# Deformable convolution on one core: bilinear weights read from a PSUM bank, the first corner add in two instructions

## The reference

```python
om = conv3x3(x, w_om, b_om)                       # offsets dy, dx and a mask for 9 taps
y0, x0 = floor(py), floor(px); fy, fx = py - y0, px - x0
sampled = corner(y0, x0, (1-fy)*(1-fx)) + corner(y0, x0+1, (1-fy)*fx) \
        + corner(y0+1, x0, fy*(1-fx)) + corner(y0+1, x0+1, fy*fx)
sampled = sampled * sigmoid(m)[:, None]
y = einsum('bckhw,ock->bohw', sampled, w) + b
x = x + relu((y - bn_mean) * scale + beta)
```

## Time and profile before

| | |
|---|---|
| three runs, median | 1822.37 us (1814.28 to 1834.46) |
| the profiled execution, its own time | 1817.64 us |
| its span in the trace | 1815.7 us |
| granted TensorE clock, mean | 0.87 of full speed |

### The profile page before, as it was taken

One profiled execution on the slowest core, in us unless ns is written; L12 is line 12 of the kernel. 1 busy time (PEld: TensorE's weight loads), 2 busy tenths in 40 slices (PEclk: granted clock), 3 DMA queues, 4 the chain that ended last, 5 costly groups with the idle time before them and its releaser, 6 DMA issues.

```text
span 1815.7 us, 13011 instructions
## 1 busy us (share of the span) xinstructions
PE 1335.5 (74%) x3820; PEld 578.4 (32%) x3820; DVE 921.6 (51%) x1344; ACT 522.2 (29%) x861; POOL 1240.9 (68%) x1393
## 2 busy tenths in 40 slices
PE   1867674896259998864599998754799754886986
PEld 1543232343124343322244333321343221332422
DVE  2345456454533435887434338975243596333165
ACT  1212121221123343211423442223234313223344
POOL 8367777767777777777777777777777777770000
PEclk9888886898579999986699999976799886997998
DMA  7022323332352222323342223222311122211000
GB/s 231 20 71 62 88 64 76 102 89 65 83 118 54 54 57 64 83 58 82 83 105 53 58 56 81 70 62 70 103 50 51 51 71 54 61 53 30 0 1 12
DMA packets 111189, 122.37 MB, mean 67 GB/s; under 512 B 50704, under 2 KB 88336, under 8 KB 110736
## 3 DMA queue, kind: packets, MB, share of 16 engines
q0 software_dynamic: 36864, 75.57, 15.6%
q1 hardware_dynamic: 73296, 42.57, 9.7%
q10 hardware_dynamic: 960, 3.41, 0.5%
HBM read 99.79 MB, written 9.08 MB: 60 GB/s over the span
## 4 chain that ended last, share of the span: by engine, by line
POOL 53%; PE 19%; issue 17%; DVE 4%; DMA 2%; SPq 2%; ACT 2%; ACTq 0%; POOLq 0%; DVEq 0%
POOL gt L936 53%; PE bank L1567 3%; PE bank L1563 3%; PE bank L1577 3%; PE bank L1688 2%; PE bank L1651 2%; PE bank L1597 2%; PE bank L1638 2%; DMA sqb<-gate_of_token 1%; PE bank L1674 1%; DVE gt L1365 1%; SPq L680 1%; PE bank L1626 1%; SPq L722 1%; DMA gate_of_token<-cw 0%
## 5 line engine op out<-in xcount | busy, mean ns | idle before, releaser
L936 POOL DMA_INDIRECT gt<-corner_table,idx x1152 | 1187.3, 1031 | 387.5 <-issue 350.2
L1365 DVE TENSOR_TENSOR gt<-gt,cw 128x1152 f32<-128x1152 f32 x128 | 173.6, 1356 | 153.7 <-DMA gt<-corner_table,idx 153.2
L1638 PE MATMUL bank<-u,wk 128*128 128x512 f32 x512 | 242.2, 618 | 11.7 <-DMA u<-sqb 6.5
L1651 PE MATMUL bank<-yg,wts 128*128 128x512 f32 x512 | 237.3, 608 | 0.3 <-DVE rb L1406 0.3
L1567 PE MATMUL bank<-xg,w_sb 128*128 128x512 f32 (+1 forms) x288 | 144.9, 587 | 82.2 <-DVE xg L1278 74.5
L1449 DVE SCALAR_TENSOR_TENSOR rb<-xp,par,rb 128x1024 f32<-128x1024 f32 x151 | 187.7, 1291 | 0.0
L1394 DVE SCALAR_TENSOR_TENSOR tg<-tg,ae 128x512 f32<-128x512 f32 x64 | 44.3, 693 | 242.6 <-ACT ae L1078 242.6
L1616 PE MATMUL bank<-cst,sm 128*128 128x128 f32 x384 | 76.7, 316 | 114.3 <-DVE sm L1371 111.8
L1287 DVE SCALAR_TENSOR_TENSOR he<-he,bank 128x512 f32<-128x512 f32 (+1 forms) x144 | 90.2, 627 | 128.8 <-PE bank L1567 123.7
L1006 ACT ACTIVATE he<-bank 128x512 f32<-128x512 f32 (+1 forms) x144 | 79.1, 549 | 248.5 <-PE bank L1563 248.1
L1563 PE MATMUL bank<-xp,w_sb 128*128 128x512 f32 (+1 forms) x288 | 142.3, 578 | 4.0 <-ACT he L1006 3.4
(11 more groups left out here) (186 smaller groups left out, 1257.5 us busy)
## 6 DMA issues: line engine op xcount, KB each, us to landing
gt<-corner_table,idx POOLq DMA_INDIRECT x1152, 2.6
tb<-gate_of_token SPq DMA_DIRECT2D x32, 256.0 KB, 5.1
sqb<-gate_of_token SPq DMA_DIRECT2D x24, 256.0 KB, 5.1
u<-sqb SPq DMA_DIRECT2D x48, 128.0 KB, 6.5
corner_table<-tb SPq DMA_DIRECT2D x36, 128.0 KB, 2.5
w_sb<-w ACTq DMA_DIRECT2D x2, 1024.0 KB, 6.7
sqb<-gate_of_token SPq DMA_DIRECT2D x16, 128.0 KB, 3.2
out<-X SPq DMA_DIRECT2D x8, 256.0 KB, 2.2
```

The costliest lines, as they stand in the source:

```text
L936: pool.indirect_dma_start(gt[:, t % GRING, k].rearrange("p a c -> p (a c)"), None, corners, bass.IndirectOffsetOnAxis(ap=idx[s % 2][:, j, ...
L1365: ch.then(tt(rows, rows, share.unsqueeze(2).to_broadcast([P, 4 * KK, C]), ALU.mult))
L1638: op = mm(psum[b][:, :], wk[:, t, d], u4[:, g, at:at + HALF], start=t == 0, stop=t == JJ - 1 and n > 0)
L1651: op = mm(psum[B2.bank(*name)][:, :], w_glu[:, k, col + d * P:col + (d + 1) * P], yg[:, c % 2, k], start=k == 0, stop=k == NB2 - 1)
```

## The change

Three edits, all in L1.

1. At the first tile of each bunch DVE copies the shares of the whole bunch (4 tiles x 1 or 2 images x 36 values) from `cw` to PSUM bank 4 with a tensor_scalar by 1.0, and each tile's multiplication reads its 36 shares from that bank in place of SBUF. `gt` stays in SBUF.
2. So bank 4 is no longer there for `dcn`: its product, the ReLU and the add to x use bank 3, the bank of the transposed samples, in turn with them.
3. The first corner add, 576 elements, becomes two instructions, of the taps 0 to 4 (320 elements) and 5 to 8 (256), with no wait between them.

```diff
             elif kind == "dcn":
-                use((4,), ("dcn", *k))
+                use((3,), ("dcn", *k))
...
             def dcn(s, m):
                 r = rows(sums(s)[m][0])
+                b = B1.bank("dcn", s, m)
                 B1.filled(act, "dcn", s, m)
-                act.activation(psum[4][r, :], psum[4][r, :], ACT.Relu, bias=bi1[r, :], scale=sc1[r, :])\
+                act.activation(psum[b][r, :], psum[b][r, :], ACT.Relu, bias=bi1[r, :], scale=sc1[r, :])\
                    .then_inc(S["relu_done"], 1)
...
                 rows = gt[:, i].rearrange("p k a c -> p (k a) c")
-                share = cw[s % 2][:, j, g * KK:(g + 1) * KK].rearrange("p k a -> p (k a)")
+                images, n = sums(s)[m]
+                w = len(images) * KK * 4
+                if j % NJ == 0 and g == images[0]:
+                    some = cw[s % 2][:, n * NJ:(n + 1) * NJ, images[0] * KK:(images[-1] + 1) * KK]
+                    ch.then(ts(psum[4][:, 0:NJ * w].rearrange("p (t k) -> p t k", t=NJ),
+                               some.rearrange("p t k a -> p t (k a)"), 1.0, None, ALU.mult))
+                at = (j % NJ * len(images) + images.index(g)) * KK * 4
+                share = psum[4][:, at:at + 4 * KK]
                 ch.then(tt(rows, rows, share.unsqueeze(2).to_broadcast([P, 4 * KK, C]), ALU.mult))
-                ch.then(tt(gt[:, i, :, 0:2], gt[:, i, :, 0:2], gt[:, i, :, 2:4], ALU.add))
+                for ks in (slice(0, 5), slice(5, KK)):
+                    ch.did(tt(gt[:, i, ks, 0:2], gt[:, i, ks, 0:2], gt[:, i, ks, 2:4], ALU.add))
+                ch.wait()
...
             def dcn(s, m):
                 B1.vacant(pe, "dcn", s, m)
+                b = B1.bank("dcn", s, m)
...
-                        op = mm(psum[4][g * C:(g + 1) * C, :], w_dcn[:, k], st[:, place_in(s, m, g), k], start=k == 0,
+                        op = mm(psum[b][g * C:(g + 1) * C, :], w_dcn[:, k], st[:, place_in(s, m, g), k], start=k == 0,
                                 stop=k == 2)
-                op.then_inc(full[4], 1)
+                op.then_inc(full[b], 1)
```

More of the change, by code:

```diff
@@ L1378, in dcn @@
                 xh = X[r, s, n * HALF:(n + 1) * HALF]
-                tt(xh, xh, psum[4][r, :], ALU.add).then_inc(free[4], 1)
+                b = B1.bank("dcn", s, m)
+                tt(xh, xh, psum[b][r, :], ALU.add).then_inc(free[b], 1)
             def l2_head(s, i):
```

## The result

| | before | changed |
|---|---|---|
| median | 1824.8 us (1814.3 to 1834.5) | 1782.3 us (1778.7 to 1783.4) |
| profiled execution | 1817.64 us, span 1815.7 | 1783.39 us, span 1781.6 |
| last indirect DMA ends | 1639.3 us | 1602.0 us |

The ratio is 0.9764 with a 95% interval of 0.9736 to 0.9792: 2.4% faster, where 1.5% was forecast (1795 us, range 1777 to 1816). Between the two profiled executions the difference is 34.3 us.

What follows compares the result with a forecast made beforehand. POOL's 1152 indirect DMAs, each row plus its pause, were taken to bound the kernel. Terms -61.9 + 27.7 + 2.7 + 2.4 + 1.5 = -27.6 us took the median from 1822.4 to 1795 us; own range 1785 to 1803, full range 1777 to 1816.

Steps and rivals of the forecast that it cites:

- part 1: L1's multiplication, reading its shares from PSUM, no longer holds any indirect DMA: -61.9 us.
- Part 2: DMAs let through wait at random moments for the split add and the sum: +27.7 us, bounds -4.9 and +57.8.
- second rival: Adds and sum take back what the multiplication gives, their moments falling badly in each tile: 1813 us, chance 0.12.
- Part 3: In two stretches, some 20 tiles, DMAs let through meet L3's taps and lose half the gain: +2.7 us.
- Part 4: From 287 to 409 us DVE and PE are behind, so POOL waits away its gain in 9 tiles: +2.4 us.
- third rival: DVE and PE become the bound, POOL meets a full ring each step, half the gain lost: 1807 us, chance 0.08.
- Part 5: DVE's extra time for add halves and copies, multiplication unchanged, is mostly covered by waits for gathers: +1.5 us.
- Part 6: Moving dcn to bank 3 costs nothing: 0 taken, upper bound 12 us of PE's time.
- Part 7: After the last gather, the tail of L2 and L3 has no POOL work and moves as a whole, staying 176 us.
- last rival: More gain than counted: the add's halves let DMAs in early and fewer meet the adds: 1777 us, chance 0.07.

Runs made afterwards that it cites:

- e3: Changed kernel with the multiplication reading its shares from cw in SBUF again, all else kept: 1824.4 us, 1.0037 of the kernel before.
- e5: Changed kernel with the first add split by corner, one half written to PSUM for the last add, shares copied per tile: 1783.1 us, 0.9786 of the kernel before.
- e9: Changed kernel with the last add reading one operand from PSUM and the first step's expert units spread over more tiles: 1775.1 us, 0.9748 of the kernel before.
- e6: Changed kernel with the first step's 32 expert units spread over tiles 16.3 to 24.0 instead of 22.5: 1772.7 us, 0.9736 of the kernel before.
- e4: Kernel before with only dcn's product moved to bank 3: 1819.2 us, 0.9999 of the kernel before.
- e8: The changed kernel run again without any edit: 1781.5 us, 0.9785 of the kernel before.
- e1: Changed kernel with the first corner add as one instruction again: 1781.1 us, 0.9802 of the kernel before.
- e10: Changed kernel with the expert units spread over more tiles and the first corner add in one piece: 1771.0 us, 0.9735 of the kernel before.

## Why the prediction was right, and where its sizes were off

The forecast was faster, 1795 us; it is 1782. The mechanism stood as argued: DMAs waited for DVE instructions with two SBUF tensors, and the multiplication's 61.9 us went to zero (part 1). e3 shows the cause by one operand: 88 DMAs held for 51.5 us with it in SBUF, none with it in PSUM. The Trainium skill says that in its probe tensor_tensor did not stall DMAs whose descriptors GpSimd makes (SBUF — State Buffer, section Who interferes with whom); for the indirect DMAs of this kernel these two runs show otherwise.

Part 2, the DMAs that meet the adds, was mis-sized: +27.7 forecast, +5.8 + 2.3 = +8.1 measured. (The squares given there make 32.4 us, not 32.6.) I had used a random moment, and the moments aren't random. In 61 of the 128 tiles of the changed kernel a DMA began in the stretch from 0.20 us before the add to 0.03 after its start and was not held; at random it would be 128 x 0.23 / 1.24 = 24.

One reason can be read from the rows. When a DVE instruction just before the multiplication holds a DMA, that DMA is released as the multiplication starts, and the next one reads 1.24 us later, while the multiplication has 1.35 us to run and the add behind it starts at 1.38. Here a tap does it:

```profile
721.64 1.27 DVE L1460 SCALAR_TENSOR_TENSOR rb<-xp,par,rb 128x1024 f32<-128x1024 f32 x1
722.11 1.62 POOL L936 DMA_INDIRECT gt<-corner_table,idx  x1 [0.30 <-issue]
722.84 1.34 DVE L1373 TENSOR_TENSOR gt<-gt,bank 128x1152 f32<-128x1152 f32 x1
724.04 0.94 POOL L936 DMA_INDIRECT gt<-corner_table,idx  x1 [0.30 <-issue]
724.21 0.83 DVE L1375 TENSOR_TENSOR gt<-gt 128x320 f32<-128x320 f32 x2
```

In 27 of the 61 tiles the DMA before was held in this way. In the other 34 it was not, so this is less than half of the explanation. The last tile but one is of these: DVE had waited 8.07 us for the gather, and nothing stood before the multiplication that could hold a DMA.

```profile
1592.21 1.35 DVE L1373 TENSOR_TENSOR gt<-gt,bank 128x1152 f32<-128x1152 f32 x1 [8.07 <-DMA gt<-corner_table,idx]
1593.43 0.94 POOL L936 DMA_INDIRECT gt<-corner_table,idx  x1 [0.30 <-issue]
1593.60 0.82 DVE L1375 TENSOR_TENSOR gt<-gt 128x320 f32<-128x320 f32 x2
1594.46 0.46 DVE L1381 TENSOR_TENSOR sm<-gt 128x288 f32<-128x288 f32 x1
1594.68 1.05 POOL L936 DMA_INDIRECT gt<-corner_table,idx  x1 [0.30 <-issue]
```

The DMA at 1593.43 passes just ahead of the add, and the one after it falls to the sum and waits 0.11 us. The counts are from the rows; no run moved the moments by themselves, and for the 34 tiles the cause stays open. It was the second rival's idea of regular moments, with the opposite sign. Its lower bound (nothing added) was nearer than the value that I took.

Part 3, the taps, was too small: +2.7 forecast, +8.4 measured. I counted half the gain of some 20 tiles, but more DMAs are held by taps than before (34 against 25), each for longer (0.69 against 0.60 us on average). One of them:

```profile
714.16 1.28 DVE L1460 SCALAR_TENSOR_TENSOR rb<-xp,par,rb 128x1024 f32<-128x1024 f32 x1
714.54 1.72 POOL L936 DMA_INDIRECT gt<-corner_table,idx  x1 [0.30 <-issue]
```

This row is 0.78 us over 0.94. e5 and e9 show it again: with the last add freed as well the taps take 25.1 and 26.9 us.

Part 4, the stretch with the full ring, was too small: +2.4 forecast, +10.2 measured. I had counted the tiles 16 to 24 alone. What POOL had gained in the tiles before was waited for as well, as the starts of the tiles' first DMAs show (tiles counted from 0; us earlier than in the trace of the kernel before):

| tile | 14 | 20 | 26 | 40 | 56 | 127 |
|---|---|---|---|---|---|---|
| changed | 8.9 | 7.6 | 0.2 | 9.2 | 13.7 | 37.3 |
| e6 | 8.9 | 8.4 | 14.9 | 20.2 | 25.8 | 48.8 |

After the stretch (tile 26 begins at about 409 us) the changed kernel has nothing left of its lead. e6 keeps it. The third rival (DVE and PE bound) was right in this one place and nowhere else.

Part 5: sizes right, 0.492 and 0.417 us for the halves, 0.455 and 0.301 for the copies, and no PSUM cost of the multiplication. By the two fixed costs in the Trainium skill (VectorE: DVE Perf Modes, section The TRN2 errata), 120 cycles from PSUM and 58 from SBUF, it would by estimate be 65 ns longer; it is 8 ns shorter. Part 6, bank 3, is nothing, as e4 shows. Part 7, the tail moves as a whole: it took 3.2 us longer, which is within what it varies by.

Parts 2 to 4 together were forecast at +32.8 and are +26.7. That they came so near is partly luck: part 2 was 19.6 us too high, parts 3 and 4 together 13.5 us too low. With the rest of the table the profiled executions differ by -34.3 us, where the sum said -27.6. The medians differ by more, 42.5 us when the result was taken and 41.4 in e8's group, since the profiled execution of the kernel before (1817.6 us) lies at the fast end of its runs; in the group of e1 to e4 its median was 1817.8. The forecast's own range, 1785 to 1803, missed the result by 3 us.

The last rival, "more than I count" with 1777 us, came nearest in time. Its reason was that the halves let DMAs in early. 18 DMAs were released at the end of a first half and 11 at the end of a second, but e1 and e10 have no halves and are as fast, so that reason doesn't carry the difference.

## What to carry to other kernels

Where GpSimd issues indirect DMAs back to back, look at the spread of their rows, not at the mean: each row that ends a fixed time after a DVE instruction (0.82 us here) names what holds it. A small operand that many long DVE instructions share can be worth a copy to PSUM: here 18 copies, 7.6 us of DVE's time, took away 61.9 us of holding, and the multiplication cost the same (1.348 against 1.356 us). When such a stall goes, the gain is paid out only as far as the other engines keep up. Here one stretch of 125 us, in which the ring had been full twice before, took back all that the first 26 tiles had gained; respacing its work belongs to the change.

## What was not expected of the hardware

- The hold is sharp: a held DMA ends 0.82 us after the end of the DVE instruction, within 0.02 us in 335 of the 344 rows over 0.965 us of the kernel before and in 195 of 205 of the changed one, and it gets in even between two DVE instructions that stand back to back without a wait (1057.37 above). A DMA that begins a few hundredths of a microsecond after the DVE instruction is ahead of it; then the DVE instruction is the longer one, by 0.06 us in these two rows of the kernel before (the multiplication has a median of 1.353 us; the six with a DMA begun up to 0.05 us after their start took 1.415 on average).

```profile
1418.57 1.41 DVE L1365 TENSOR_TENSOR gt<-gt,cw 128x1152 f32<-128x1152 f32 x1 [3.60 <-DMA gt<-corner_table,idx]
1418.59 0.94 POOL L936 DMA_INDIRECT gt<-corner_table,idx  x1 [0.30 <-issue]
```

- "Two SBUF tensors" is not the whole condition. The group norm's L1307, a tensor_scalar that reads one tensor (and two scalars per partition) from SBUF and writes to SBUF, holds DMAs too: all that began beside it, four or five in each of the twelve traces. In the row below the DMA ends 0.82 us after 431.95. The tensor_scalar that copies the shares (L1369, from SBUF to PSUM) held none of the four that began beside it in the changed kernel. What sets the two apart was not tried.

```profile
431.14 0.81 DVE L1307 TENSOR_SCALAR xpad<-X,mv,rs 128x1024 f32<-128x1024 f32 x1
431.51 1.26 POOL L936 DMA_INDIRECT gt<-corner_table,idx  x1 [0.30 <-issue]
```

- Taking a hold away shifts all later moments, so what one instruction gave up others took in part: 61.9 us freed, 16.5 taken by adds, sum and taps.
- The runs of the changed kernel lie closer together than those of the kernel before (4.7 against 20.2 us from lowest to highest when the result was taken, four runs each). In the later groups the kernel before spread over 9.2, 14.3 and 7.8 us, and the changed kernel over 4.8. Why was not tried.
